# Reordering the copy of the aggregated sums in the node stage of a two-layer graph network kernel

## The reference

```python
edge_index = jnp.stack([src, dst])
h = jnp.maximum(_layernorm(x), 0.0)
# first layer
edge_feat = jnp.concatenate([h[src], h[dst], edge_attr], axis=-1)
messages = mish(mish(edge_feat @ W1 + b1) @ W2 + b2)
agg = segment_sum(messages, dst, 1250)
u = mish(jnp.concatenate([h, agg], axis=-1) @ W3 + b3)      # the node stage starts here
y = h + (u @ W4 + b4)
x = x + layernorm(y) * gamma + beta
# second layer
h = jnp.maximum(_layernorm(x), 0.0)
support = ((h @ U) * s) @ Vt
x = x + relu(segment_sum(support[src] * edge_weight[:, None], dst, 1250) + bias)
```

## Time and profile before

| what | value |
|---|---|
| timed runs, median (lowest, highest) | 1547.55 us (1547.35, 1548.13) |
| profiled execution, its own time | 1548.88 us |
| profiled execution, span from the first to the last instruction | 1547.2 us |
| mean granted clock of TensorE over the span | 0.989 of full speed |
| node stage and final stage | from about 1409 us to the end of the span |
| PE busy in 1400 to 1547.2 | 133.6 of 147.2 us |

### The profile page before, as it was taken

The page is one execution under the profiler, slowest core; times in us unless marked ns, Lnnn a source line. Parts: engine busy times, 40 slices in busy tenths (PEclk is TensorE's granted clock), DMA queues, the critical chain, the costliest instruction groups (busy, mean ns, idle before and its releaser), DMA issues.

```text
span 1547.2 us, 33384 instructions
## 1 busy us (share of the span) xinstructions
PE 1502.3 (97%) x7862; PEld 1172.1 (76%) x7862; DVE 1418.2 (92%) x2922; ACT 1297.7 (84%) x2505; POOL 1080.3 (70%) x984
## 2 busy tenths in 40 slices
PE   7869999999999999999999999999999999999998
PEld 5657777777777777777777777777777777776785
DVE  7579999999999999999999999999999999995666
ACT  4049999999999999999999999999999999986352
POOL 1236878888878788887888887888887887752220
PEclk9979999999999999999999999999999999999999
DMA  8854555555555555554555555554554555544663
GB/s 275 322 181 107 125 123 116 124 123 116 124 123 116 122 124 116 122 124 114 125 121 115 126 117 117 127 119 116 127 117 117 128 118 117 135 107 125 136 144 152
DMA packets 122451, 205.09 MB, mean 133 GB/s; under 512 B 31641, under 2 KB 54297, under 8 KB 122416
## 3 DMA queue, kind: packets, MB, share of 16 engines
q0 software_dynamic: 59392, 116.85, 35.1%
q1 hardware_dynamic: 63024, 87.83, 18.7%
HBM read 151.60 MB, written 42.75 MB: 126 GB/s over the span
## 4 chain that ended last, share of the span: by engine, by line
PE 79%; issue 5%; DVE 5%; POOL 4%; DMA 3%; ACT 1%; POOLq 1%; SPq 0%; DVEq 0%; ACTq 0%
PE bm L1069 47%; PE bp L1048 6%; PE bp L1056 5%; PE bs L1092 4%; PE bp L1058 4%; PE pm L1080 2%; PE po L2008 2%; PE pu L1986 2%; PE pA L678 1%; DMA xg<-A_tab,idx 1%; PE pm L1079 1%; PE pu L335 1%; POOL hTl L975 1%; PE pB L678 1%; POOL M_tab L1000 1%
## 5 line engine op out<-in xcount | busy, mean ns | idle before, releaser
L975 POOL TENSOR_TENSOR hTl<-tp,hTh 128x512 fp32r<-128x512 f32 (+1 forms) x314 | 411.2, 1309 | 231.4 <-DVE khl L1251 203.4
L1069 PE MATMUL bm<-W2h,hTh 128*128 128x512 f32 x1252 | 498.3, 398 | 2.9 <-POOL hTl L975 2.3
L1069 PE MATMUL bm<-W2l,hTh 128*128 128x512 f32 x1252 | 497.2, 397 | 0.0
L1069 PE MATMUL bm<-W2h,hTl 128*128 128x512 f32 x1252 | 494.6, 395 | 0.0
L964 POOL DMA_INDIRECT xg<-A_tab,idx x305 | 319.2, 1047 | 49.8 <-issue 37.0
L1069 PEld LDWEIGHTS bm<-W2h,hTh 128*128 128x128 f32 x1252 | 235.5, 188 | 72.9 <-DVE bm L1244 15.1
L1129 ACT ACTIVATE rp<-bp 128x512 f32<-128x512 f32 (+1 forms) x314 | 183.8, 585 | 120.3 <-PE bp L1058 118.9
L1069 PEld LDWEIGHTS bm<-W2l,hTh 128*128 128x128 f32 x1252 | 235.5, 188 | 57.5
L1069 PEld LDWEIGHTS bm<-W2h,hTl 128*128 128x128 f32 x1252 | 235.6, 188 | 53.4
L1215 DVE SCALAR_TENSOR_TENSOR rp<-rp 128x512 f32<-128x512 f32 (+1 forms) x314 | 215.3, 686 | 34.6 <-ACT rp L1129 22.3
L1225 DVE SCALAR_TENSOR_TENSOR tp<-rp,bp 128x512 f32<-128x512 f32 (+1 forms) x314 | 211.4, 673 | 3.2 <-ACT rp L1135 0.8
(11 more groups left out here) (244 smaller groups left out, 2327.7 us busy)
## 6 DMA issues: line engine op xcount, KB each, us to landing
ea<-in_eaT SPq DMA_DIRECT2D x156, 128.0 KB
M_tab<-mev POOLq DMA_DIRECT2D x157, 80.0 KB
agg_tab<-ev POOLq DMA_DIRECT2D x157, 64.0 KB
db<-in_dst_rows SPq DMA_DIRECT2D x78, 128.0 KB
M<-M SPq DMA_DIRECT2D x78, 128.0 KB
eaW<-Bh_tab SPq DMA_DIRECT2D x79, 64.0 KB
eaW<-Bl_tab SPq DMA_DIRECT2D x79, 64.0 KB
xg<-A_tab,idx POOLq DMA_INDIRECT x313
```

Source lines behind the costliest of these rows:

```text
L975: e.tensor_tensor(hTl[p][:, j, 0:w], pick(u, start_t, tp)[:, 0:w], hTh[p][:, j, 0:w], ALU.subtract)\
L1069: last = e.matmul(bank[0:r, :], a[p][:, c, j * P:j * P + r], w[:, c, :], start=False, stop=c == KC - 1 and w is W2l, skip_group_check=True)
```

## The change

Two edits in the order of two streams; no instruction is added, removed or changed in shape.

```diff
@@ ACT
             make_h(0)
-            for f in range(KC):
+            for f in range(KC - 1):
                 chain(0, f)
             evac_agg(1, 0)
+            chain(0, 3)
             evac_agg(1, 1)
             chain(1, 0)
@@ DVE
             cap(0, 3)
             mish(0, 2)
+            lo_agg(1, 0)
             mish(0, 3)
-            lo_agg(1, 0)
             lo_agg(1, 1)
             seeds_bias()
@@ DVE
             mish(1, 2)
             cap(1, 3)
+            lo_agg(2, 0)
             second_norm(1)
-            lo_agg(2, 0)
             mish(1, 3)
             cap(2, 0)
```

## The result

| | before | changed |
|---|---|---|
| median of 12 runs | 1547.68 us | 1545.0 us |
| lowest, highest | 1544.69, 1550.36 | 1542.83, 1547.08 |
| ratio | | 0.9984, 95% interval 0.9977 to 0.9991 |

The change saves 0.16%, about 2.5 us (1.4 to 3.6). The forecast was 2.0 us, 1545.5. The profiled execution of the changed kernel took 1547.08 us with a span of 1545.4, near the top of its runs; so the traces are compared stretch by stretch and not by their spans.

A forecast was written before the change was run, and what follows sets the result against it. PE, busy 97%, was held to be bound by a pause behind xpart(1, 0), with a smaller one at h2_T(0). 1547.55 - 1.62 - 0.39, clock counted 0, gave 1545.5 us, range 1543.4 to 1547.4.

The forecast's parts named there:

- What bounds it: PE idles 3.29 us behind xpart(1, 0) for chunk 4's low part; DVE's mish(0, 2) ahead of it waits for POOL's lo(0, 0).
- First term: At DVE's mish(0, 3): chunk 4's low part goes ahead of it and starts 1.62 us earlier, shortening PE's pause by that.
- The pause left over: PE's pause behind xpart(1, 0), before chunk 6's transposes, shrinks from 3.29 to 1.67 us.
- The clock: Behind the chunk 6 pause: full clock returns, worth 1.4 us in the profiled execution, counted 0 for the median.
- clock in the median: Rival: timed runs also lose 1.4 us to the lower clock behind the long pause and regain it; 1544.1, chance 25%.
- more clock: Rival: the low stretch behind 1487.45 goes too, another 1.5 us, near 1542.6; chance 5%.
- Hidden costs: Delayed chain(0, 3), 0.9 us later, stays covered; low parts beside POOL keep 1.27; apart(1, 0) has 0.9 us spare.
- Third term: At h2_T(0): low parts moved ahead of DVE's refinement remove PE's pause of 0.39 us.
- Sum: Whole kernel: 1547.55 - 1.62 - 0.39 = 1545.5 for the median; chance 0.60 of staying within 0.2%.
- slower rival: Light 128x64 PE stretches, moved by 2 us, fall to the lower clock; two more give +1.0, 1548.6; chance 7%.

The follow-up runs named there:

- e5: Kernel before with POOL's lo(0, 0) and lo(0, 1) ahead of the DMA issues of add_b4_beta(0), none of the change's edits; ratio 0.9984, saves 2.5 us.
- e2: Kernel before with only the low parts of chunks 8 and 9 moved ahead of DVE's refinement (second_norm(1)); ratio 1.0004, saves -0.6 us.
- e9: Kernel before, unchanged, traced a second time; one execution, no ratio; pause at chunk 6 2.78 us.
- e4: Changed kernel with POOL's lo(0, 0) and lo(0, 1) ahead of the DMA issues of add_b4_beta(0); ratio 0.9962, saves 5.9 us against before.
- e6: Kernel before with ten unused 128x512 matmuls added in PE's pause behind xpart(1, 0); ratio 0.9981, saves 2.9 us.
- e8: Kernel before with only the ACT edit, copies of chunks 4 and 5 ahead of chain(0, 3); ratio 0.9995, saves 0.8 us.
- e1: Kernel before with the ACT edit and DVE's low parts of chunks 4 and 5 ahead of mish(0, 3); ratio 0.9980, saves 3.1 us.
- e3: Kernel before with only DVE's low parts of chunks 4 and 5 ahead of mish(0, 3), ACT as before; ratio 0.9997, saves 0.5 us.
- e11: Changed kernel with six unused 128x512 matmuls added behind xpart(1, 0); ratio 0.9975, saves 3.9 us against before.

## Why the prediction was right

- **What bounds it.** Right: PE stood at chunk 6 for a low part behind two mishes, the first released by POOL and not by ACT as the view of before had it. The changed kernel's trace names POOL, and e5 moves POOL alone and gains. It is not the only course, though: in e2 and e9 a cast beside POOL delays ACT's last chain, and in e4, e5, e6 and e8 POOL is on time and `mish(0, 3)` waits for that chain. I had one trace and took its course for all.
- **First term, 1.62 us.** Measured 1.63 between `mish(0, 2)` and the low part, in both traces of the change and in e1, and e1 carries the whole gain. That the total agrees is in part luck: I wrote that all other pauses have causes that the change doesn't touch, yet the early pause is missing in this build, and what it gave is not separated from the order's share.
- **The pause left over.** Wrong in size: 2.31 and 2.88 us, not 1.67. I held POOL and PE at the offset of one execution; POOL's end varies with the landing of the edge stage's last writes, and in this build PE arrives earlier, by 1.5 us in one trace and 0.6 in the other.
- **The clock.** I counted 0 for the median and expected full clock behind the pause. Both were wrong. Both traces of before have the low stretch, and e6's time and mean clock say that filling the pause takes it away in the median too; both traces of the changed kernel keep it, behind 2.31 and 2.88 us. The two errors offset each other, which was luck: what was not lost by my account was not regained either. The rival "clock in the median" (1544.1) had the loss right and its return wrong; the measured 1545.0 lies between that and the forecast. As to "more clock", the low stretch behind 1487.45 stayed in one trace of the change and was missing in the other, behind the same pause of 1.34 us.
- **Hidden costs.** Right in this trace: `chain(0, 3)` moved by 0.8 us relative to its cap and nobody waited; the pair beside POOL kept 1.27; no pause in front of `apart(1, 0)`. I priced the ACT edit at nothing either way. Where POOL is on time it is not hidden: alone it cost 0.83 us there (e8). And the copies that it moves are what the low part would wait for in the second and third course, by the order of the work; e3's shortfall fits that.
- **Third term, 0.39 us.** Right in the trace, too small for the timing (e2).
- **Sum.** 2.0 forecast, 2.5 (1.4 to 3.6) measured, within 0.2% of no change, as given the larger chance. The slower rival did not come: no new low stretch appears behind 1490.

## What to carry to other kernels

When an engine stands behind a wait for two semaphores, look in the code for which count each needs: here the count that was needed of the named one had been reached 3.4 us before. Then look at the engine that really is late, since moving its work (here two DMA issues behind two small products) can be worth as much as reordering around it (2.5 us each here), and both together more (5.9). Take a second trace before pricing a wait that depends on a DMA's landing. And when two builds differ by 2 us, compare them piece by piece: here a pause far in front of the edits had come or gone.

## What the runs showed of the hardware

At chunk 6 a pause of 2.1 us or more was followed by some 3.4 us at 1.2 GHz in every trace, one of 1.5 us or less in none. Length alone is not the rule: the early pause, with transposes just ahead of it, was followed by the lower level in e4 (2.77 us), e5 (1.94), e6 (1.93) and e8 (1.94), and not in e2 and e11 (2.21 each) or before, e9 and e3 (1.93 each). A pause of 1.34 us behind 128x64 matmuls was followed by it in eight traces and not in four, among these the second trace of the changed kernel. Ten unused matmuls in a pause made the program faster (e6, 2.9 us). DVE's cast of 128x512, 0.43 us alone, took 3.23 and 3.54 us where it ran beside POOL's DMA issues and product, while the subtraction from PSUM with one SBUF input kept its 0.64 us beside POOL. And that early pause of 1.9 to 2.8 us, shortly behind the start of the node stage, was there in some builds and missing in others with the same PE instructions; the two traces of before agree, and so do the two of the changed kernel, and its cause stays open.
